# Two cross-attention layers over keys on the partitions: where queries and contexts are split within a step, when the last tile's maxima and outputs are turned, and one output scaled ahead of a copy

## The reference

```python
def _cross_attention(q_in, kv_in, wq, bq, wk, bk, wv, bv, wo, bo, bias_k, bias_v):   # H, K = 16, 128
    qh = (q_in @ wq + bq).reshape(b, q_len, H, K)
    kh = (kv_in @ wk + bk).reshape(b, t, H, K)
    vh = (kv_in @ wv + bv).reshape(b, t, H, K)
    kh = jnp.concatenate([kh, jnp.broadcast_to(bias_k, (b, 1, H, K))], axis=1)
    vh = jnp.concatenate([vh, jnp.broadcast_to(bias_v, (b, 1, H, K))], axis=1)
    logits = jnp.einsum('bqhk,bthk->bhqt', qh, kh) / scale
    weights = jax.nn.softmax(logits, axis=-1)
    ctx = jnp.einsum('bhqt,bthk->bqhk', weights, vh).reshape(b, q_len, H * K)
    return ctx @ wo + bo
```

## Time and profile before

| | |
|---|---|
| median of three runs | 1940.74 us (1938.85 to 1943.6) |
| profiled execution, its own time | 1938.15 us |
| its span | 1936.4 us, granted TensorE clock 0.962 |
| TensorE busy | 1695.1 us, 88% |
| TensorE weight loads | 1585.4 us, 82% |
| VectorE busy | 1247.1 us, 64% |
| ScalarE busy | 1034.7 us, 53% |
| GpSimd busy | 914.8 us, 47% |

### The profile page before, as it was taken

The page is one execution under the profiler, slowest core; times in us unless marked ns, Lnnn a source line. Parts: engine busy times, 40 slices in busy tenths (PEclk is TensorE's granted clock), DMA queues, the critical chain, the costliest instruction groups (busy, mean ns, idle before and its releaser), DMA issues. The chain is left out here.

```text
span 1936.4 us, 40609 instructions
## 1 busy us (share of the span) xinstructions
PE 1695.1 (88%) x12516; PEld 1585.4 (82%) x12516; DVE 1247.1 (64%) x2350; ACT 1034.7 (53%) x2021; POOL 914.8 (47%) x688
## 2 busy tenths in 40 slices
PE   3689888876789998998998988899899899899897
PEld 3677777765579998998998987789899899899886
DVE  6577777756576566665665666866666666666664
ACT  2467666656355454555555555636546445545463
POOL 4445555523354534534534537554354453453473
PEclk8899999999899999999999999999999999999998
DMA  7777667554140100100100102411010010010021
GB/s 228 184 184 179 161 171 173 149 126 110 56 99 33 65 32 31 63 32 32 63 32 32 64 24 79 120 67 41 25 63 36 28 63 33 31 63 0 1 74 48
DMA packets 113943, 149.65 MB, mean 77 GB/s; under 512 B 25476, under 2 KB 99716, under 8 KB 113860
## 3 DMA queue, kind: packets, MB, share of 16 engines
q1 hardware_dynamic: 112516, 142.42, 26.7%
q10 hardware_dynamic: 1344, 6.19, 1.0%
HBM read 108.28 MB, written 3.42 MB: 58 GB/s over the span
## 5 line engine op out<-in xcount | busy, mean ns | idle before, releaser
L713 POOL TENSOR_TENSOR rr<-ar,rr 125x512 fp32r<-125x512 f32 x336 | 454.9, 1387 | 492.1 <-ACT rr L1443 343.7
L1008 PE MATMUL ps<-cx,rr 125*128 125x258 f32 x1344 | 405.0, 301 | 0.0
L1010 PE MATMUL ps<-cx,rr 125*128 125x256 f32 x1344 | 385.7, 287 | 0.0
L1012 PE MATMUL ps<-cx,rr 125*128 125x258 f32 x1344 | 385.5, 287 | 0.0
L761 PE MATMUL ps<-rr,ct 128*125 128x256 f32 x1152 | 329.9, 286 | 7.9 <-DVE ar L1838 6.1
L763 PE MATMUL ps<-rr,ct 128*125 128x256 f32 x1152 | 324.7, 282 | 0.0
L762 PE MATMUL ps<-rr,ct 128*125 128x256 f32 x1152 | 324.5, 282 | 0.0
L1008 PEld LDWEIGHTS ps<-cx,rr 125*128 125x128 f32 x1344 | 261.3, 194 | 1.8 <-issue 0.2
L1010 PEld LDWEIGHTS ps<-cx,rr 125*128 125x128 f32 x1344 | 262.2, 195 | 0.0
L1012 PEld LDWEIGHTS ps<-cx,rr 125*128 125x128 f32 x1344 | 261.7, 195 | 0.0
L1430 ACT ACTIVATE ar<-ar 125x512 f32<-125x512 f32 x336 | 208.0, 626 | 93.4 <-DVE ar L1838 72.0
(11 more groups left out here) (202 smaller groups left out, 3802.3 us busy)
## 6 DMA issues: line engine op xcount, KB each, us to landing
raw_t<-in_ctx_t SPq DMA_DIRECT2D x24, 1500.0 KB, 6.7
k<-khl SPq DMA_DIRECT2D x192, 187.5 KB
raw<-in_ctx SPq DMA_DIRECT2D x16, 1500.0 KB
raw<-in_ctx SPq DMA_DIRECT2D x8, 1408.0 KB
raw<-stat_scratch ACTq DMA_DIRECT2D x7, 750.0 KB, 3.9
w_raw<-in_wq SPq DMA_DIRECT2D x32, 128.0 KB, 2.5
w_raw<-in_wk SPq DMA_DIRECT2D x32, 128.0 KB, 2.9
w_raw<-in_wv SPq DMA_DIRECT2D x32, 128.0 KB, 2.2
```

The lines of the kernel that those rows point to most:

```text
L713: pool.tensor_tensor(group(p[:, 1, :, :], u, k), x, f(group(p[:, 0, :, :], u, k)), ALU.subtract)\
L1008: pe.matmul(ps[:, bank, 0:D + 2], hi, cx[0:KC, c, 0:D + 2], start=c == 0, stop=False, skip_group_check=True)
L1010: pe.matmul(ps[:, bank, 0:D], hi, cx[0:KC, c, D + 2:CW], start=False, stop=False, skip_group_check=True)
L1012: mm = pe.matmul(ps[:, bank, 0:D + 2], lo, cx[0:KC, c, 0:D + 2], start=False, stop=c == CH - 1, skip_group_check=True)
```

## The change

Six things move; no instruction of an engine with a time of its own is added or taken away.

1. On TensorE, where nu is the single tile, the last output of the unit before is turned after four banks of scores, not two.
2. On TensorE, the turning and spreading of the maxima stand after 6 and 11 chunks where nu is the single tile, after 3 and 8 where u is the single tile, and after 4 and 9 as before between pairs.
3. On ScalarE, a pair's step splits the queries of the unit after next behind the low halves of the scores, not first of all. The three context splits follow all six `low_scores`.
4. On ScalarE, the second output of a pair is scaled ahead of the high copy of the fifth group (`k == 4`), not behind it. Where nu is the single tile it stays behind the third.
5. On VectorE, the third context part of a batch (`split_cx`) is split behind the second maximum of step (b, 0), not before the first; the queries are split in the shift (behind the third group between pairs, behind the first where nu is the single tile), or, where u is the single tile, behind all maxima.
6. On VectorE, where nu is the single tile, the shift's three groups each have a context split behind them, and the sums come behind the first of these, ahead of the queries' split.

```diff
--- before.py
+++ after.py
@@ -961,7 +961,7 @@
                         pe.wait_ge(s["ct_hi"], 3 * bc + j // 2 + 1)
                         pe.wait_ge(s["ct_lo"], 3 * bc + j // 2 + 1)
                     scores(i, b, u, j)
-                    if j == 1:
+                    if j == (1 if pair(u) else 3):
                         between()
 
             def turn_max(i, b, u, o_before):
@@ -1147,13 +1147,15 @@
                         turn_before()
                     if not first:
                         pe.wait_ge(s["o_back"], tiles(i, b, u) - (1 if pair(before[1]) else 0))
-                    weighted(i, b, u, 0, range(0, 4))
+
+                    first_at, next_at = (6, CH - 1) if not pair(nu) else (4, 9) if pair(u) else (3, 8)
+                    weighted(i, b, u, 0, range(0, first_at))
                     if not end:
                         turn_max(i, nb, nu, o_before())
-                    weighted(i, b, u, 0, range(4, 9))
+                    weighted(i, b, u, 0, range(first_at, next_at))
                     if not end:
                         spread_max(i, nb, nu)
-                    weighted(i, b, u, 0, range(9, CH))
+                    weighted(i, b, u, 0, range(next_at, CH))
                     if pair(u):
                         pe.wait_ge(s["m_ready"], units(i, nb, nu) + 1)
                         weighted(i, b, u, 1, range(0, 6))
@@ -1479,7 +1481,7 @@
                     end = last and not pair(u)
                     (nb, nu), before = after(b, u), after(b, u, -1)
                     later = after(b, u, 2)
-                    if not (last and u >= UNITS - 2):
+                    if not pair(u) and not end:
                         split_q(i, *later)
                     if not (zero(b) and u == 0):
                         turn_output(i, *before, 1 if pair(before[1]) else 0)
@@ -1493,8 +1495,11 @@
                         context = (i + 1, 0) if last else (i, b + 1)
                         for j in range(CH // 2):
                             low_scores(i, nb, nu, j)
-                            if j % 2 and follows:
-                                split_ct(*context, j // 2)
+                        if follows:
+                            for j in range(3):
+                                split_ct(*context, j)
+                    if pair(u) and not (last and not pair(nu)):
+                        split_q(i, *later)
                     if not pair(u):
                         split_cx(i, nb, 0)
                         split_cx(i, nb, 1)
@@ -1509,11 +1514,13 @@
                             split_cx(i, nb, 2)
                         if k == 0:
                             scale_output(i, b, u, 0)
+                        if k == 4 and pair(u):
+                            scale_output(i, b, u, 1)
                         high_probs(i, nb, nu, k)
-                        if k == min(2, GROUPS[nu] - 1) and pair(u):
+                        if k == 2 and pair(u):
                             turn_output(i, b, u, 0)
-                        if k == min(4, GROUPS[nu] - 1) and pair(u):
-                            scale_output(i, b, u, 1)
+                            if not pair(nu):
+                                scale_output(i, b, u, 1)
 
                 whole_layer(act, step)
 
@@ -1774,7 +1781,7 @@
                 hi, lo = (q[:, 0, :, :], q[:, 1, :, :]) if pair(u) else (q[:, :, 0, :], q[:, :, 1, :])
                 dve.tensor_tensor(lo, src, f(hi), ALU.subtract).then_inc(s["q_lo"], 1)
 
-            def running_max(i, b, u, order=range(CH // 2), between=()):
+            def running_max(i, b, u, order=range(CH // 2), between=None):
 
                 n, steps = units(i, b, u), maxima(i, b, u)
                 done = 0
@@ -1805,8 +1812,8 @@
                             dve.wait_ge(s["s_free"], CH // 2 * n + 6)
                             dve.tensor_tensor(run[0:KC, :], run[0:KC, :], group(xp, u, 2), ALU.max)\
                                 .then_inc(s["run_max"], 1)
-                    if m < len(between):
-                        between[m]()
+                    if between is not None:
+                        between(m)
 
             def row_max(i, b, u):
 
@@ -1822,7 +1829,7 @@
                 dve.tensor_tensor(negm[:, 0:count], mx2[:, 0:count], nlbq[:, bass.ds(g, count)], ALU.min)\
                     .then_inc(s["neg_ready"], 1)
 
-            def shift(i, b, u, between=()):
+            def shift(i, b, u, between=None):
                 n, count = units(i, b, u), 2 if pair(u) else 1
                 dve.wait_ge(s["max_b"], n + 1)
                 dve.tensor_copy(m_b[0:KC, 0:P * count], ps[0:KC, 7, 0:P * count]).then_inc(s["m_ready"], 1)
@@ -1838,8 +1845,8 @@
                         dve.tensor_tensor(x, src, m, ALU.add).then_inc(s["s_free"], 1)
                     else:
                         dve.tensor_tensor(x, x, m, ALU.add).then_inc(s["shifted"], 1)
-                    if k < len(between) and between[k] is not None:
-                        between[k]()
+                    if between is not None:
+                        between(k)
 
             def sums(i, b, u, t):
                 n, g = tiles(i, b, u) + t, TILES * b + 2 * u + t
@@ -1897,19 +1904,24 @@
                         sums(i, b, u, 0)
                         extra_probs(i, 1)
                         return
-                    if u == 0:
-                        split_cx(i, b)
-                    queries = () if last and u >= UNITS - 2 else (lambda: split_q(i, *later),)
-                    running_max(i, nb, nu, between=queries)
-                    follows = not pair(nu) and (not last or i == 1)
-                    context = (i + 1, 0) if last else (i, b + 1)
-                    if follows:
-                        split_ct(*context, 0)
+                    def beside_maxima(m):
+                        if u == 0 and m == 1:
+                            split_cx(i, b)
+
+                    def beside_shift(k):
+
+                        if not pair(nu) and (not last or i == 1):
+                            split_ct(*((i + 1, 0) if last else (i, b + 1)), k)
+                        if k == (1 if pair(nu) else 0):
+                            sums(i, b, u, 0)
+                        if k == (2 if pair(nu) else 0) and pair(u) and not (last and u >= UNITS - 2):
+                            split_q(i, *later)
+
+                    running_max(i, nb, nu, between=beside_maxima)
+                    if not pair(u):
+                        split_q(i, *later)
                     row_max(i, nb, nu)
-                    shift(i, nb, nu, (None, lambda: sums(i, b, u, 0)))
-                    if follows:
-                        split_ct(*context, 1)
-                        split_ct(*context, 2)
+                    shift(i, nb, nu, beside_shift)
                     if last and u == 1:
                         extra_values(i)
                     if last and u == UNITS - 2:
```

## The result

The changed kernel takes 1889.3 us (median of 4 runs, 1888.0 to 1892.3) against 1942.1 before (also 4 runs, one more than in the median of 1940.74): ratio 0.973, interval 0.971 to 0.975. That is 2.7% faster; 1.6% was forecast. The profiled execution has a span of 1888.1 us, 48.3 less than before.

A forecast was written before the change was run, and what follows sets the result against it. TensorE was taken to bound the kernel, only its own gaps costing. 46.3 + 1.1 + 19.0 + 19.7 + 4.2 + 4 - 43.5 - 17.5 - 3 = 30.3 us off 1940.7 gave 1911, range 1885 to 1934.

The forecast's parts named there:

- the long stall: TensorE's L975 waiting for a pair's maxima in step (b, 0), 3.3 us, 14 times: would go, gaining 46.3 us.
- steps (b, 0) and (b, 1): Multiplying a batch's units 0 and 1, scoring the next: 46.3 us gained from L975's wait, 3 us of new waits lost.
- step (b, 2): Multiplying unit 2, scoring the single tile: 19.7 us gained up to the first output's turning, 43.5 lost to a new stall.
- step (b, 3): Multiplying the single tile, scoring the next unit: L761's wait goes, 14 x 0.3 = 4.2 us gained.
- slow stretches at these stalls: TensorE at 1.2 GHz for 3.41 us, costing 1.46 each: 13 go (19.0 us), 12 come (17.5 us).
- layers' first steps and last batches: Same L975 wait in the two steps (0, 0), 1.1 us gained; L988 and clock in last batches, 4 us gained.
- the new waits taken off for GpSimd and the late exponentials: In steps (b, 0) and (b, 1), waits for GpSimd's L713 and later exponentials: 3 us lost, bounds 0 and 14.
- The new stall: In step (b, 2), TensorE's L988 waits for ScalarE's L1450: 3.1 us, 14 times, 43.5 us; bounds 2.3 and 3.9.
- A: Rival: the new stall in step (b, 2) leaves the clock alone, 17.5 us less, 1893; chance 0.20.
- B: Rival: no new stall in step (b, 2), exponential and shift have more slack; gain 91 us, 1850; chance 0.04.
- C: Rival: clock stays low for three stretches after each L988 stall in step (b, 2), 1955; chance 0.07.
- D: Rival: no change to be told, two slow stretches after each new stall, 1934; chance 0.11.

The follow-up runs named there:

- the two single edits: Kernel before with VectorE's queries' split alone moved into the shift, 1872.1 us; kernel before with its context split alone moved behind the second maximum, 1975.9 us.
- the longer stall: Changed kernel with two context splits instead of one between the first two groups of the single tile's shift: 1917.7 us.
- the fastest version: Changed kernel, single tile's first two shift groups back to back, sums then queries' split later, one context split ahead of the maxima's reduction, two behind the shift: 1853.2 us.
- two other runs with the same stall: Changed kernel with the queries' split behind the sixth group between pairs, 1910.7 us; changed kernel with the second output scaled behind the copy again, 1890.6 us.
- the split beside GpSimd: Changed kernel with VectorE's queries' split behind the sixth group of the shift between pairs, not the third: 1910.7 us in one run.

## Why the prediction was right, and where its sizes were off

The direction and both main mechanisms were right, the long stall that goes and the new one that comes; the gain was sized at 30.3 us where the attention gained 54.7. By parts, with the steps' lengths at full clock times 14, and 1.46 us for a slow stretch:

| part | forecast | measured |
|---|---|---|
| steps (b, 0) and (b, 1) | +46.3 - 3 = +43.3 | +52.4 |
| step (b, 2) | +19.7 - 43.5 = -23.8 | -17.3 |
| step (b, 3) | +4.2 | +4.9 |
| slow stretches at these stalls | +19.0 - 17.5 = +1.5 (13 to 12) | +11.7 (13 to 5) |
| layers' first steps and last batches | +1.1 + 4 = +5.1 | the rest, +3.0 |
| sum | 30.3 | 54.7 |

*The long stall of step (b, 0)*: right in mechanism. 47.5 us of L975's waits went, and none of the 13 slow stretches is left at that place. It was the queries' split alone, as the two single edits show; the prediction let both splits leave the path together. Step (b, 0) takes 18.34 us, 22.04 before, so 3.70 went where the list shows 3.29. The list counts a wait from the shown end of the last matmul, which lies 0.16 us behind the time at which the next could be issued; that is 2 of the 9 us by which the first row is off. Another 3 are the new waits taken off for GpSimd and the late exponentials: they did not come (step (b, 1) takes 18.22, 18.27 before). What makes the remaining 4 stays open.

*Step (b, 2) up to the first output*: TensorE could issue its turning 13.70 us after the step's first score, 15.06 before (its last matmul ahead of it starts at 632.23, and the next could follow 0.12 later): 1.4 us gained a step, as forecast. L975 waits 0.49 (0.7 forecast), the wait behind L981 is 0.2 (0.3). But it is not TensorE's new order that gains this, as the forecast had it in part: that order alone shortens step (b, 2) by 0.1 us, and the fastest version loses nothing there without it (16.15 for 16.35). The gain comes with the new lists of ScalarE and VectorE; no run tells which of the two.

*The new stall*: here is the term that was mis-sized. The mechanism was right, and the longer stall shows that it is paid one for one (1.11 us more in the trace for one more split). The list shows 2.36 us, 33.0 in all, where the sum had 3.1 and 43.5; counted as the sum counts, from 632.35 to 634.87, it is 2.5. The sum's chain from the end of the maxima's copy to the end of L1450 was 5.3 us, measured 4.8, and the whole of these 0.5 is the queries' split: 0.85 us from the sums' end to its own, where the sum had 1.35 from the 1.46 of the earlier trace rows. That row was taken beside a running L713, of which 0.91 us were left, and at the new place GpSimd is idle (for 11.80 us, until its L713 at 636.18): 0.69. The range of 2.3 to 3.9 for the stall held the value. TensorE's last matmul ahead of the stall:

```profile
632.23 0.28 PE L1012 MATMUL ps<-cx,rr 125*128 125x258 f32 x1
```

The prediction had the rule for it in hand, and used it for GpSimd's loss at L1768, not for VectorE's own duration.

*The clock after the new stall*: 5 slow stretches, 12 in the sum, 7.3 us for 17.5. The sum took the rate of the old stall of 3.3 us, and the new one is shorter: at 3.5 us it is 14 of 14, at 3.3 it was 12 of 14, at 2.36 it is 5. That it is 5 is in part chance: two other runs with the same stall have 7 and 8.

*Step (b, 3)*: 13.76 us, 14.11 before; 0.3 as forecast.

*The rivals*: A (the clock stays full) was nearer than the forecast, with 1893, but not for its reason: 5 stretches came, and the stall was shorter than it took, and the two nearly cancel. B (no new stall) is refuted by the 2.36 us and by the run that takes this stall away. C and D did not come, and the longer stall shows that even 3.5 us brings one stretch and not three.

## What to carry to other kernels

An instruction in a strictly ordered queue can cost what it waits for rather than what it takes (here 3.06 us of waiting ahead of a split that takes 0.69 alone): look first for the one that waits for another engine ahead of work that is ready, and move that one alone. Before pricing an instruction at a new place, look at what the neighbouring engine did beside it in the row that the price comes from, and what it does at the new place. And a move that ends a long stall may open a shorter one by what it is moved in front of; follow the release of the next buffer through both engines.

## What the runs showed of the hardware

VectorE and GpSimd in turns: the 512-wide queries' split (two inputs in SBUF) takes 0.68 to 0.69 us with no L713 running, in all 108 such cases of five profiles (before, the changed kernel, the two single splits, the split beside GpSimd). When it begins during an L713 it ends 0.54 to 0.55 us after that L713 ends, in 119 of 132 cases, whether 1.25 us of the L713 were left (it took 1.79), 0.91 (1.46), 0.41 (0.95) or 0.27 (0.82). The other 13 began less than 0.07 us before the end of an L713 and took 1.80 to 1.86: the next L713 went first. GpSimd is held up in turn (three L713 took 5.76 for 3.9 beside three context splits, and these 5.62 for 3.6). The Trainium skill (SBUF — State Buffer, "Who interferes with whom") calls what such a pair shares an exclusive lock; these numbers agree.

How often TensorE's clock is at 1.2 GHz (a granted clock of 0.50) around the end of a stall, in this loop: after 1.54 us in 0 of 14, 2.36 in 5, 7 and 8 of 14 (three profiles), 3.3 in 12 of 14, 3.5 in 14 of 14; and 3.83 us (the run with the context split alone) had 6.83 us of it 13 times of 14. The length is not the whole of it: with TensorE's positions alone, where a wait of 1.4 us stands some 36 us ahead, the same 3.3 us have a slow stretch in 14 of 14, and two in 7. Only the longer stall changes the length and little else.
